# Two changes to a six-stage metaformer kernel: the pieces in which pictures are loaded, and the order of the root operations in the modulation stage

## The reference, cut to what matters

```
x = x + L1_conv(_ln_c(x))              # first half of layer 1
  y = einsum(x, Wf) + bf                # query, context, gates
  ... depthwise convolutions of context -> ctx_all
  modulator = einsum(ctx_all, Wh) + bh
  x_out = q * modulator
  mu, var = mean(x_out, -1), mean(square(x_out - mu), -1)
  x_out = (x_out - mu) * rsqrt(var + 1e-3) * gamma + beta
  x_out = einsum(x_out, Wp) + bp
t = t + L1_ffn(_ln_t(t))               # second half: batch norm over all tokens, then a scan
```

## Time and profile before

| what | value |
|---|---|
| median of 3 runs | 13002.87 us (12997.03 to 13009.24) |
| the profiled execution, its own time | 13003.63 us |
| its span | 13001.8 us |
| mean granted TensorE clock | 0.842 of full speed |
| busy share of the span: PE, DVE, ACT, POOL | 66%, 50%, 35%, 43% |
| focal input stage, modulation stage | about 2535 and 2714 us of the span |

### The profile page before, as it was taken

The page is one execution under the profiler, slowest core; times in us unless marked ns, Lnnn a source line. Parts: engine busy times, 40 slices in busy tenths (PEclk is TensorE's granted clock), DMA queues, the critical chain, the costliest instruction groups (busy, mean ns, idle before and its releaser), DMA issues. The chain is left out here.

```text
span 13001.8 us, 325709 instructions
## 1 busy us (share of the span) xinstructions
PE 8644.4 (66%) x109727; PEld 5499.5 (42%) x109727; DVE 6469.0 (50%) x21703; ACT 4556.1 (35%) x12677; POOL 5573.7 (43%) x6829
## 2 busy tenths in 40 slices
PE   8999988888883222222269999834444444788888
PEld 6777753333332111111135555423333333455554
DVE  8999988888884111111125555523333333222222
ACT  5666655555552211111223333312222222233333
POOL 8888877777773111111112222112222222444444
PEclk9999999999997666666689999966666666899999
DMA  1222211111111111111144444322222222122222
GB/s 54 58 58 58 57 53 49 49 49 49 49 49 41 65 64 64 64 64 64 64 143 157 157 156 156 121 73 78 78 79 79 79 79 70 51 56 56 57 56 54
DMA packets 795890, 960.00 MB, mean 74 GB/s; under 512 B 321322, under 2 KB 660075, under 8 KB 771820
## 3 DMA queue, kind: packets, MB, share of 16 engines
q1 hardware_dynamic: 795500, 956.24, 23.5%
HBM read 576.90 MB, written 455.45 MB: 79 GB/s over the span
## 5 line engine op out<-in xcount | busy, mean ns | idle before, releaser
L944 PE MATMUL moe_pe_out<-moe_we,moe_xnT 128*128 128x512 f32 x3136 | 1535.7, 624 | 369.4 <-DVE moe_odd L837 195.9
L1248 PE MATMUL foc_px<-foc_idn,foc_xn 112*128 112x112 f32 x896 | 145.7, 292 | 1930.2 <-POOL foc_xn L1106 1864.6
L1920 PE MATMUL mod_pz<-mod_wpx,mod_yT 128*112 128x129 f32 x1792 | 478.9, 365 | 1377.2 <-DVE mod_xin L1824 1376.7
L1544 PE MATMUL conv_pc<-conv_c,conv_toep 128*128 128x432 f32 (+1 forms) x3584 | 1371.0, 535 | 0.0
L741 ACT ACTIVATE moe_scaled<-moe_pe_out,moe_gate 128x128 f32<-128x128 f32 x3136 | 891.9, 367 | 867.3 <-PE moe_pe_out L944 865.5
L1185 DVE BATCH_NORM_STATS2 foc_stat<-foc_xin 112x6 f32<-112x128 f32 x896 | 191.0, 276 | 1865.4 <-DMA foc_xin<-x 1865.4
L1750 ACT ACTIVATE mod_z<-mod_xin,mod_nmean,mod_rstd 112x128 f32<-112x128 f32 x896 | 368.9, 483 | 1996.2 <-DVE mod_nmean L1851 1947.1
L944 PEld LDWEIGHTS moe_pe_out<-moe_we,moe_xnT 128*128 128x128 f32 x3136 | 558.2, 195 | 1187.9 <-issue 1187.2
L2100 ACT ACTIVATE rec_yT<-rec_ph 128x32 f32<-128x32 f32 x3136 | 618.3, 197 | 1240.2 <-PE rec_ph L2221 1240.2
L1106 POOL TENSOR_SCALAR foc_xn<-foc_xin,foc_rstd,foc_nmean 112x127 f32<-112x127 f32 x448 | 202.5, 462 | 1886.2 <-DVE foc_nmean L1198 1884.4
L1406 POOL TENSOR_TENSOR conv_g<-conv_c,conv_gate 128x896 f32<-128x896 f32 x128 | 365.5, 2855 | 1474.6 <-DVE conv_out L1507 1371.0
(11 more groups left out here) (202 smaller groups left out, 21764.3 us busy)
## 6 DMA issues: line engine op xcount, KB each, us to landing
conv_toep<-rows_dram SPq DMA_DIRECT2D x32, 2304.0 KB, 14.0
c<-foc_cs SPq DMA_DIRECT2D x32, 1856.0 KB, 7.2
conv_cin<-c SPq DMA_DIRECT2D x32, 1856.0 KB, 9.0
ctx_all<-conv_out SPq DMA_DIRECT2D x32, 1792.0 KB, 6.5
att_xin<-x_windows SPq DMA_DIRECT2D x512, 98.0 KB
x<-att_x1s SPq DMA_DIRECT2D x1024, 49.0 KB
moe_xin<-x SPq DMA_DIRECT2D x112, 448.0 KB, 3.6
x<-moe_acc SPq DMA_DIRECT2D x112, 448.0 KB, 2.7
```

Of the source, the lines that this page charges most:

```text
L944: ins = pe.matmul(pe_out[:, b, half, :], xnT[:, n.slot(2), t, :], we[:, half * 4:half * 4 + 4, :].rearrange("d e c -> d (e c)"), start=Tru ...
L1544: ins = pe.matmul(pc[k][:, half, 0:HALF * wide].rearrange("p (b i) -> p b i", i=wide)[:, :, i0:i1], w, tile[:, b, i0 + away:i1 + away], st ...
L1920: pe.matmul(pz[0:TOK, b, t, 0:C + 1], tile_of(yT, m, c, t), wpx[:], start=True, stop=True)
```

## The change

`load_quads` loads each half in three DMAs, of 48, 5 and 3 rows, instead of 3 and 53, so a picture takes six DMAs and its semaphore is waited for at 16 times 6. In the modulation stage, one power takes y's variance of step n + 1 together with x's variance of step n - 1 (before: of step n). DVE's step n becomes gate(n + 9), y's mean of n + 1, negate(n - 2), y's mean square, x's variance of n - 1, y's variance of n + 1, and only then residual, x_parts and x_statistics of n. `negate`, z (ACT) and the Gram matrix (PE) each move a step later, to n - 2, n - 2 and n - 3, and after the last step one more power and one more of each is drained. GpSimd takes `roots` of n + 1 ahead of `add_bias` of n + 2. The number of matmuls, ACT and DVE operations is the same; there is one power more in all.

```diff
--- before.py
+++ after.py
@@ -980,7 +980,7 @@
 def load_quads(eng, dst, src, n, sem):
     for half in range(2):
-        for row, real, rows in ((IMG - SHIFT, 0, SHIFT), (0, SHIFT, IMG - SHIFT)):
+        for row, real, rows in ((0, SHIFT, 48), (48, SHIFT + 48, 5), (IMG - SHIFT, 0, SHIFT)):
             p0 = half * IMG + real
             eng.dma_start(dst[p0:p0 + rows, :, :].rearrange("p k c -> p (k c)"),
                           dram(src, n.val(PIX * C, (half * IMG + row) * TILES * C), [(TILES * C, rows), (1, TILES * C)]))\
@@ -1176,7 +1176,7 @@
             def layer_stats(n, first):
                 m, c = image(n)
                 if c == 0:
-                    hold(dve, x_in[m.slot(2)], m.turn(2, 16 * 4, 16 * 4), ticks)
+                    hold(dve, x_in[m.slot(2)], m.turn(2, 16 * 6, 16 * 6), ticks)
                 if first >= 7:
                     hold(dve, rstd_done, n.val(1, -6), ticks)
                 if first >= 2:
@@ -1700,26 +1700,28 @@
             def add_bias(n):
                 m, c = image(n)
                 if c == 0:
-                    pool.wait_ge(x_in[m.slot(2)], m.turn(2, 16 * 4, 16 * 4))
+                    pool.wait_ge(x_in[m.slot(2)], m.turn(2, 16 * 6, 16 * 6))
                 x = xin[:, m.slot(2), GRP * c:GRP * c + GRP, :]
                 pool.tensor_tensor(x, x, brow[0:TOK, :].unsqueeze(1).to_broadcast([TOK, GRP, C]), ALU.add)\
                     .then_inc(x_biased, 1)
 
             def roots(n, first):
 
-                if first >= 3:
-                    hold(pool, z_normed, n.val(1, -2), ticks)
+                if first >= 4:
+                    hold(pool, z_normed, n.val(1, -3), ticks)
                 hold(pool, varied, n.val(1, 1), ticks)
                 pool.tensor_tensor(rstd[:, n.slot(2), :], var[:, n.slot(2), :], halfneg[0:TOK, :], ALU.pow).then_inc(rstd_done, 1)
 
             def step(n, first, last):
                 if first == 0:
                     add_bias(n)
+                    roots(n, 0)
                     add_bias(n + 1)
-                    roots(n, 0)
+                roots(n + 1, first + 1)
                 if last < -2:
                     add_bias(n + 2)
-                roots(n + 1, first + 1)
+                if last == -1:
+                    roots(n + 2, first + 2)
 
             run_steps(pool, N, U, step, AHEAD)
 
@@ -1745,10 +1747,10 @@
                 hold(act, nmean_done, n.val(1, 1), ticks)
                 if first >= 2:
                     hold(act, gram_added, n.val(1, -1), ticks)
-                b, r = n.slot(2), (n + 1).slot(2)
+                b = n.slot(2)
                 for t in range(GRP):
                     ins = act.activation(z[:, b, t, 0:C], xin[:, m.slot(2), GRP * c + t, :], ACT.Identity,
-                                         bias=nmean[:, b, t:t + 1], scale=rstd[:, r, GRP + t:GRP + t + 1])
+                                         bias=nmean[:, b, t:t + 1], scale=rstd[:, b, GRP + t:GRP + t + 1])
                 ins.then_inc(z_normed, 1)
 
             def step(n, first, last):
@@ -1761,9 +1763,10 @@
                     context_out(n + 10, first + 10)
                 if last < -8:
                     square(n + 8)
-                if first >= 1:
+                if first >= 2:
+                    norm_z(n - 2, first - 2)
+                if last == -1:
                     norm_z(n - 1, first - 1)
-                if last == -1:
                     norm_z(n, first)
 
             run_steps(act, N, U, step, AHEAD)
@@ -1840,16 +1843,15 @@
 
             def x_variance(n):
                 hold(dve, stats, n.val(1, 1), ticks)
-                dve.tensor_scalar(var[:, (n + 1).slot(2), GRP:2 * GRP], mv[:, n.slot(2), :, 1], EPS_T, None, ALU.add)\
-                   .then_inc(varied, 1)
+                return dve.tensor_scalar(var[:, n.slot(2), GRP:2 * GRP], mv[:, n.slot(2), :, 1], EPS_T, None, ALU.add)
 
             def negate(n, first):
                 b = n.slot(2)
-                hold(dve, rstd_done, n.val(1, 2), ticks)
+                hold(dve, rstd_done, n.val(1, 3), ticks)
                 if first >= 2:
                     hold(dve, z_normed, n.val(1, -1), ticks)
                 dve.scalar_tensor_tensor(out=nmean[:, b, :], in0=mv[:, b, :, 0], scalar=-1.0,
-                                         in1=rstd[:, (n + 1).slot(2), GRP:2 * GRP], op0=ALU.mult, op1=ALU.mult)\
+                                         in1=rstd[:, b, GRP:2 * GRP], op0=ALU.mult, op1=ALU.mult)\
                    .then_inc(nmean_done, 1)
 
             def step(n, first, last):
@@ -1861,19 +1863,23 @@
                     y_variance(n).then_inc(varied, 1)
                 if last < -9:
                     gate(n + 9, first + 9)
-                if first >= 1:
-                    negate(n - 1, first - 1)
-                residual(n)
                 if last < -1:
                     y_mean(n + 1)
-                x_parts(n)
+                if first >= 2:
+                    negate(n - 2, first - 2)
                 if last < -1:
                     y_mean_square(n + 1)
+                if first >= 1:
+                    ins = x_variance(n - 1)
+                if last < -1:
+                    ins = y_variance(n + 1)
+                ins.then_inc(varied, 1)
+                residual(n)
+                x_parts(n)
                 x_statistics(n)
-                if last < -1:
-                    y_variance(n + 1)
-                x_variance(n)
                 if last == -1:
+                    x_variance(n).then_inc(varied, 1)
+                    negate(n - 1, first - 1)
                     negate(n, first)
 
             run_steps(dve, N, U, step, AHEAD)
@@ -1941,11 +1947,11 @@
                     project(n + 1, first + 1)
                 if last < -9:
                     modulator(n + 9, first + 9)
-                if first >= 2:
-                    gram_of(n - 2, first - 2, last - 2)
+                if first >= 3:
+                    gram_of(n - 3, first - 3, last - 3)
                 if last == -1:
-                    gram_of(n - 1, first - 1, last - 1)
-                    gram_of(n, first, last)
+                    for k in (2, 1, 0):
+                        gram_of(n - k, first - k, last - k)
 
             run_steps(pe, N, U, step, AHEAD)
```

## The result

The changed kernel takes 10464.92 us (median of 4 runs, 10452.25 to 10483.84); the kernel before takes 13003.25 in the same session. The ratio is 0.8049, with a 95% interval of 0.8035 to 0.8063: 2538 us less, where 2903 were forecast. The profiled execution took 10452.25 us, span 10450.5. The sum of the prediction was 10102, so 350 us of it are missing.

What follows compares the result with a forecast made beforehand. The prediction took waits for the load of x, carried by one DMA engine, to bound both changed stages. From 13003.6 us it took 1639 for focal input and 1263 for modulation: 10102, predicted as 10100, range 9790 to 10450.

Steps and rivals of the forecast that it cites:

- What bounds the kernel, and that the load is not spread: Both changed stages: waits for the load of x, 3167 of 13002 us; one DMA engine carries it at 27 GB/s.
- The load, once spread: Load of x per picture: busiest engine's time falls from 57 to 5.3 us, bounds 3.7 and some 15.
- the one measured rate of a single engine: Spread load: 27 GB/s, measured with one engine carrying the load, used for the busiest engine's 143 kB.
- Focal input stage, the rest: Focal input stage: landing to q store 10.5 us, 135 us saved at its start, extra issues hidden under stores.
- Modulation stage, the waits: Modulation stage: add_bias's wait for the load goes altogether, and 50 us are saved at the stage's start.
- Modulation stage, the step: Modulation stage: 6.2 us a step, bound by the residual-to-residual chain through TensorE and gate; saves 1216 us with the waits.
- the sentence that gave the mix: Modulation step: clock 22% of the time at the lower level; one step in six at 8.2 us, others 5.8, give 6.2.
- The rearrangement by itself is worth about nothing: Modulation stage: the power's chain and TensorE's chain are nearly equally long, so the new order alone gains about nothing.
- (b): Modulation stage: TensorE mostly at half clock, steps of 7.2 to 8.2 us add 215 to 430 us: 10320 to 10530; 14%.
- (c): Both stages reach compute bounds, 20.8 us a picture and 5.7 us a step, 305 us less: 9800; 16%.
- (d): Load not spread, still over 60 us; its later issue in the modulation stage costs 180 us more: 13180; 4%.
- (e): Load not spread and its later issue in the modulation stage hidden: no change; 1%.

Runs made afterwards that it cites:

- the loads alone: Kernel before the change with only the new load pieces of 48, 5 and 3 rows, old modulation order kept: 10334.91 us, ratio 0.7943.
- e2_mod: Changed kernel with the old load pieces of 3 and 53 rows, so only the new modulation order: 12912.57 us, ratio 0.9923.
- e3_fill: Changed kernel plus eight bf16 filler matmuls in TensorE's pause in each modulation step, ahead of project: 10246.51 us, ratio 0.787.
- e7_order: Changed kernel with residual moved first in VectorE's modulation step and gate after the variances: 9914.62 us, ratio 0.7624.

## Why the prediction was wrong where it was

**What bounds the kernel, and that the load is not spread:** right. One engine at 27 GB/s was the cause, and 48 rows fell on all of them: the share went from 0.06 to 0.9.

**"The load, once spread":** the failed term of the focal input stage. It was forecast at 5.3 us, with 15 as the upper bound. It moved in some 12 (from 4554 to 4566 in the windows above). The step that failed is that each engine keeps "the one measured rate of a single engine": sixteen on neighbouring partitions got 10.7 GB/s each and not 27, so their six rows each took some 8 us and not 3.2. The four rows more that the busiest engines carry took 4 us and not 2.1. The row that I leaned on for the full rate, the stores of the earlier trace rows, has 128 partitions and goes to DRAM, and the load writes 48 partitions at a time. (The other bound, 3.7 us, was taken from the busiest engine's 1548 kB; the whole picture is 112 rows, 1606 kB, 3.9 us. Nothing hung on it.) From q store to landing it is 6.2 us more than forecast, from landing to q store 0.7 less, and so the distance to my terms is 33.0 - 27.6 = 5.4 us, times 29 periods: **157 us** of the 350.

**Focal input stage, the rest:** right within 1 us a picture. Landing to q store was 9.4 to 9.8 against 10.5, which hides a part of the load's error; and the start: the first q store fell from 4216.3 to 4082.4, 134 us against 135. The extra issues cost nothing, as said (4.45 us for six, before 4.09 for four).

**Modulation stage, the waits:** right. The loads land in time, add_bias waits for the first alone, and the first power comes 55 us into the stage instead of 101: 46 us against 50.

**Modulation stage, the step:** wrong by 0.78 us, and the step that failed is the sentence that gave the mix. The chain was right (5.8 at full clock, 5.94 measured; 8.2 at half, 8.33 measured), and so was that it would bind. But I took 22% of the time at the lower level from the one window of the earlier trace rows, the first quiet run of steps. It is 50%, and with that my own two terms give 6.8 us: 0.6 of the 0.78. Another 0.14 is that both terms were a little short; the rest stays open. Two other runs of steps of the kernel before, between load waits, would have told me:

```profile
9603.00:9645.00 42.00, 36.17 (x210) 31.09 (x210) 26.86 (x136) 17.15 (x41) 16.05 (x11) 0.79 0.43 106
9684.00:9728.00 44.00, 36.03 (x196) 31.59 (x197) 27.76 (x137) 17.77 (x42) 16.76 (x12) 0.73 0.41 102
```

At 0.79 and 0.73 they hold the levels of the loads alone (0.79) and of the kernel after (0.75). The clock was also read off the old order and put onto the new one, where it is lower still (0.75 against 0.79 with the same loads). Powers over 1382 us were forecast, with 3 more for the drain, and 1569.9 measured: **185 us** too few. With 157, the 4 of this stage's start and 1 of the other's, that makes 347 of the 350.

**"The rearrangement by itself is worth about nothing":** right at the full clock (6.00 against 6.06 us a step) and wrong on the chip as it runs: 130 us slower beside the new loads, 97 faster beside the old. The sentence weighed the two chains at the full clock alone. At the lower level they are not equal, 7.52 us in the old order and 8.33 in the new, and the share of the time at that level is not the same either: 0.79 in the old order and 0.75 in the new.

**The rivals.** (b), TensorE at half clock most of the time, was the nearest: 6.98 us a step, just under the 7.2 from which I had counted it. That and the mis-sized load came together, and the range had counted them one at a time; so it ended 15 us short of the result. (c) did not come, since neither bound of compute was reached. (d) and (e), not spread, did not come either, and e2_mod tested (d)'s price: with the loads unspread, the rearrangement gives 97 us back where (d) charged 180.

## What to carry to other kernels

A transfer that one DMA engine carries is worth cutting into a piece that spreads, but its new rate is to be taken from a row with the same partitions, not from one that spans 128. Where a wait is removed from a stage in which TensorE pauses in every step, read the granted clock in several quiet stretches and take the whole spread into the range: at 0.75 or at 0.98 the same step took 6.98 or 6.00 us here. Compare two orders at both levels of the clock, since another chain can bind at each. And when work is moved off one chain, ask which operations of the moved group the next chain really needs, and put those first: the same operations in another order were worth 550 us.

## What the runs showed of the hardware that was not expected

- The spread load keeps nearly all of the 16 DMA engines busy and moves 136 to 172 GB/s, while a DMA of 112 rows across both halves moves 330 to 354 at a similar share. A share near 1 is no sign of the full rate.
- Eight extra matmuls in each step made the stage faster: 218 us less for e3_fill, the clock 0.98 instead of 0.75. For the loads alone the gain was 78 us.
- Beside GpSimd's add_bias, the variance's first operation, one input of 4 columns in SBUF, took 1.21 us in e7_order, where it takes 0.17 in the median. I had counted such a stretching only for negate, with its two inputs. From VectorE's timeline in that run:

```profile
7512.01 1.21 DVE L1846 TENSOR_SCALAR mod_var<-mod_mv 112x4 f32<-112x4 f32 x1
```
